# A two-layer attention and mixture-of-experts kernel whose first experts' stage issues no dummy products on TensorE

## The reference, cut to what matters

```python
logits = xf @ router_w.T                      # 256 features -> 64 experts
scores = softmax(logits); topk_w, topk_idx = top_k(scores, 8)
...                                           # each expert collects at most CAP = 64 token slots
gate = einsum('ech,ehf->ecf', xb, w_gate)     # h = 256, f = 96
up   = einsum('ech,ehf->ecf', xb, w_up)
hmid = silu(gate) * up
yb   = einsum('ecf,efh->ech', hmid, w_down)
out  = zeros.at[slot_token].add(yb[dest] * topk_w)
...
x = x + s * silu(out)                         # layer 0 ends; layer 1 works on the same x
```

## Time and profile before

| | us |
|---|---|
| median of 3 executions | 1122.3 |
| lowest and highest of them | 1118.9, 1123.69 |
| the profiled execution, its time | 1118.6 |
| its span in the trace | 1116.6 |
| TensorE busy | 988.5 |
| VectorE busy | 851.8 |
| ScalarE busy | 667.4 |
| GpSimd busy | 544.5 |
| mean granted TensorE clock | 0.955 |

### The profile page before, as it was taken

The page is one execution under the profiler, slowest core; times in us unless marked ns, Lnnn a source line. Parts: engine busy times, 40 slices in busy tenths (PEclk is TensorE's granted clock), DMA queues, the critical chain, the costliest instruction groups (busy, mean ns, idle before and its releaser), DMA issues.

```text
span 1116.6 us, 22230 instructions
## 1 busy us (share of the span) xinstructions
PE 988.5 (89%) x6749; PEld 650.3 (58%) x6749; DVE 851.8 (76%) x2241; ACT 667.4 (60%) x1739; POOL 544.5 (49%) x538
## 2 busy tenths in 40 slices
PE   3967879856999999999999999999988899999985
PEld 2535533334565676666666766767654678885443
DVE  4787548846798779768668899999856887775777
ACT  1733425524768766977866666666646877775332
POOL 0489556621755565544444444544521345553774
PEclk9987989976999999999999999999999999999997
DMA  9979699879562466121211001210049345553443
GB/s 340 338 220 368 161 261 289 287 259 279 81 166 76 115 117 144 36 74 39 63 53 39 32 8 39 91 39 1 1 135 322 98 134 145 147 139 92 133 131 95
DMA packets 97023, 155.99 MB, mean 140 GB/s; under 512 B 12272, under 2 KB 67312, under 8 KB 94096
## 3 DMA queue, kind: packets, MB, share of 16 engines
q1 hardware_dynamic: 77184, 115.42, 31.5%
q0 software_dynamic: 19728, 39.21, 15.8%
HBM read 104.84 MB, written 45.02 MB: 134 GB/s over the span
## 4 chain that ended last, share of the span: by engine, by line
PE 56%; DVE 14%; ACT 9%; issue 6%; DMA 4%; POOL 4%; DVEq 4%; POOLq 1%; ACTq 1%; SPq 0%
PE ps L1094 9%; PE ps L1266 6%; PE ps L1158 5%; PE ps L1146 5%; PE ps L1108 5%; PE ps L1126 3%; PE ps L1212 3%; PE ps L1229 3%; ACT arena L1522 2%; PE ps L1284 2%; PE ps L991 1%; PE ps L1136 1%; PE ps L1008 1%; PE ps L1256 1%; DVE x_sb L1909 1%
## 5 line engine op out<-in xcount | busy, mean ns | idle before, releaser
L2354 POOL TENSOR_TENSOR arena<-arena 128x512 f32<-128x512 f32 x128 | 174.6, 1421 | 98.3 <-ACT arena L1499 98.2
L1094 PE MATMUL ps<-arena 128*128 128x512 f16 x768 | 178.4, 383 | 1.3 <-ACT arena L1499 1.3
L2359 POOL TENSOR_TENSOR arena<-arena 128x512 f32<-128x512 f32 x64 | 67.7, 1057 | 176.0 <-DVE arena L2003 176.0
L2396 POOL DMA_INDIRECT wvo<-xn_d,idx x79 | 75.7, 958 | 113.5 <-PE ps L1256 96.4
L1094 PEld LDWEIGHTS ps<-arena 128*128 128x128 f16 x768 | 75.3, 98 | 93.9 <-ACT arena L1499 3.5
L1522 ACT ACTIVATE arena<-arena 128x128 f32<-128x128 f32 x256 | 99.2, 390 | 38.6 <-DVEq L1998 38.6
L1498 ACT ACTIVATE arena<-ps 64x512 f32<-64x512 f32 x128 | 76.0, 593 | 52.0 <-DVE arena L1971 48.4
L1158 PE MATMUL ps<-wvo,arena 128*128 128x256 f16 x768 | 95.1, 276 | 6.0 <-DVE s_sb L2023 3.2
L1146 PE MATMUL ps<-arena 128*128 128x192 f32 (+1 forms) x512 | 94.5, 328 | 2.4 <-DVE arena L2009 2.4
L1971 DVE TENSOR_TENSOR arena<-ps,wvo 128x512 f32<-128x512 f32 x128 | 84.7, 684 | 15.0 <-PE ps L1094 14.4
L1108 PE MATMUL ps<-wvo,arena 128*128 128x512 f16 x384 | 93.0, 379 | 2.9 <-issue 1.5
(11 more groups left out here) (296 smaller groups left out, 2193.6 us busy)
## 6 DMA issues: line engine op xcount, KB each, us to landing
arena<-wqk_d SPq DMA_DIRECT2D x16, 1024.0 KB, 5.8
arena<-in_wgu SPq DMA_DIRECT2D x32, 384.0 KB, 3.8
y_d<-wvo SPq DMA_DIRECT2D x79, 128.0 KB, 2.4
z_d<-wvo SPq DMA_DIRECT2D x8, 1024.0 KB, 4.3
z_d<-wvo SPq DMA_DIRECT2D x2, 4096.0 KB, 25.6
arena<-in_wdn SPq DMA_DIRECT2D x32, 192.0 KB, 5.3
arena<-z_d SPq DMA_DIRECT2D x12, 512.0 KB, 4.1
arena<-z_d POOLq DMA_DIRECT2D x12, 512.0 KB, 6.7
```

Of the source, the lines that this page charges most:

```text
L1094: last = pe.matmul(ps[s][:, :], wqk[gg][:, s * DC + c, w, hh * DH:(hh + 1) * DH], hx[bb][:, :, x, c * P:(c + 1) * P], start=(c == 0 and w ...
L2354: nc.gpsimd.tensor_tensor(qk_s[:, s], qk_s[:, s], sin, ALU.mult).then_inc(sin_done, 1)
```

## The change

`keep_clock` and its one call are deleted. Everything else is as before, on all engines: the same products, waits, transfers, buffers. In the kernel after, line numbers behind the deleted helper are 5 lower, and behind the deleted call 6 lower.

```diff
-            def keep_clock(bank, n):
-
-                for _ in range(n):
-                    pe.matmul(ps[bank][:, :], ones_bf[:, :], ones_bf[:, :].unsqueeze(1).to_broadcast([P, 4, P]), start=True, stop=True)
...
             def expert_turn(j):
 
                 upto(pe, hmT_rd, j - 1)
-                keep_clock(6, 2)
                 upto(pe, hm_ready, j)
                 pe.transpose(ps[6][0:F0, 0:P], hm0[:, j % 4], ident[:, :]).then_inc(hmT_ps, 1)
```

## The result

| | before | after |
|---|---|---|
| median, us | 1121.07 (4 executions) | 1143.42 (4 executions) |
| all executions, us | 1118.9, 1119.85, 1122.3, 1123.69 | 1128.13, 1141.65, 1145.19, 1146.23 |
| mean granted clock of these of after | | 0.933, 0.918, 0.911, 0.913 |
| profiled execution: time, span | 1118.6, 1116.6 | 1141.65, 1139.7 |

With all four, median over median is 1.020. The forecast was 1146 us, between 1116 and 1150, slower.

What follows compares the result with a forecast made beforehand. The prediction took TensorE to bound the kernel, at its clock's pace: low after the stall, 105.9 us replace 81.4 (+24.5), tail -1.0, net +23.5; 1122.3 + 23.5 = 1146 us, range 1116 to 1150.

Steps and rivals of the forecast that it cites:

- The clock decides, not the removed work: Experts' stage: the edit's price is which clock the rounds get, not the 64 products removed; net +23.5 us.
- Once low, it stays low until the stage ends: Experts' stage after the stall: TensorE's clock stays at 0.50 to the end; 1146 us, chance 0.53.
- the prediction's own sign: Test on the profile after: a granted clock going to and fro in the experts' stage would mean rival B.
- rival B: Experts' stage: the clock returns, but late; 1124 to 1138 us, say 1130; chance 0.19.
- Prices of rounds: Experts' stage, rounds without dummies: one unit 4.03 us low, 2.42 high; double rounds 8.6 low, 6.4 high.
- The dummies before the stall: Six rounds before the wait for pair 8's rows: removing 12 dummies gains 0 us, bounds 0 and -0.4.
- The sum from there: From the restart after the stall to the end of TensorE's stage work: 105.9 us at the low clock, before 81.4.
- The tail: From TensorE's stage end to the last scatter: 2.3 us before, about 1.4 at the slow pace, so -1.0.
- This goes to the end undiminished: Behind the experts' stage everything hangs on the last scatter, so the net +23.5 us reaches the kernel's end.
- Rival A: Experts' stage: the clock returns 9.07 us after the restart and stays; -6.9 us, 1115 us; chance 0.20.
- rival C: Experts' stage: the clock returns but DMA or VectorE takes up the freed time; 1120 to 1123 us; chance 0.08.
- once high, no stretch of the stage comes near the pause that brought it down: Argument for Rival A: behind the restart, no stretch resembles the 144.90 to 151.11 pause, so the clock holds.

Runs made afterwards that it cites:

- e4: Kernel before with its two dummies only in turns 13 to 24, the twelve rounds of the double stretch: median 1127.8 us, ratio 1.006.
- e5: Kernel before, its dummies moving the same 512 columns over 32 rows and 32 weight columns in place of 128 and 128: ratio 1.037.
- e8: Kernel after, unchanged, ten more executions on another chip: median 1167.8 us against 1149.9 for the kernel before, ratio 1.010.
- e1: Kernel after plus 26 filling products with ones in TensorE's idle stretch at the end of round 4: median 1137.2 us, ratio 1.018.
- e3: Kernel before with one dummy per pair in place of two: median 1116.7 us, ratio 0.9986.
- e6: Kernel after plus 26 filling products at the end of round 4 and two dummies before the middle unit's product in six double rounds: ratio 1.0005.
- e10: Kernel before plus 26 filling products in round 4's idle stretch, one dummy per pair, two before the middle unit's product in six rounds: 1112.1 us, ratio 0.9945.

## Why the prediction was right, point by point

**The clock decides, not the removed work: right.** e4 and e5 show it from both sides: with dummies put back in 12 of the 32 pairs the clock is held there, with dummies as long on a sixteenth of the array it is at 0.50 throughout. e8 shows the total time following the clock from one execution to the next.

**"Once low, it stays low until the stage ends": right in kind, too strong.** In the profiled execution it rose at 179 and at 209 us and fell again 10 and 3.5 us later; that saved 4.0 us in the double rounds (rounds 12 to 23 took 226.62 - 178.99 = 47.6 us, 51.6 forecast). In e8 it did stay low. By the prediction's own sign ("if the clock goes to and fro, B") the profiled execution is in part rival B, at nearly the forecast's price, since only 13.4 of 102.6 us were high; and the fastest execution, 1128.1 us, lies in B's 1124 to 1138. What lifts the clock in rounds that look alike in the timeline is open; it differs from execution to execution, and so does the time.

**Prices of rounds: right.** One unit, low level: 4.03 forecast, 4.07 measured. Double, low: 8.60 and 203.27 - 194.59 = 8.68. Double, high, no dummies: 6.4 and 187.02 - 180.59 = 6.43. One unit, high, no dummies: 2.42 forecast; 2.40 where the transfers had slack (e4), **2.81 where they had not** (e1).

**The dummies before the stall: 0 to -0.4 us.** TensorE's first transposes behind the pause start at 150.74, before at 151.11: -0.4, the lower bound. Pair 8's rows were indeed asked for earlier (L2321 at 137.59, before L2327 at 138.08). But the prediction took them for what ends the pause, and in this trace the transfer that TensorE waits for is `short_d`, which landed at 150.15; in e8 it waits for both, 5.14 and 1.52 us. The two are close, and the prediction named only one. The sum from there: 105.9 us forecast, 252.76 - 150.74 = 102.0 measured. The tail took 1.7 us where I had 1.4. Together +19.6 at the last scatter instead of +23.5.

**"This goes to the end undiminished": right, and the total was met by luck.** The total of the profiled pair, +23.1, meets the forecast of +23.5 only because 3.5 us came later, in unchanged work, where the profiled execution of the kernel before was quicker than every later one (881.7 us against 883.0 to 887.7). The stage itself cost 19.6. Here two errors cancel.

**Rival A** rested on two claims that fell. Its -6.9 contained 3.0 us for rounds with one unit, 0.30 each. In e1 they were slower than with dummies, as long as the weights' transfers were behind; in e3, which came nearer to A's case, six rounds took 170.19 - 154.16 = 16.0 us, 2.67 each, with DMA at 1.04, so little came back there either. What I had put into rival C at 0.08 is a part of A. And "once high, no stretch of the stage comes near the pause that brought it down" was wrong: the clock fell behind waits of 1.1 to 1.3 us among rounds without dummies (after, e1, e6), far shorter than the pause.

**Of the rule in the Trainium skill, "TensorE: Matmul & The Clock Gate", section "What's actually happening"**, that sustained activity releases the throttle, the runs show the limit: 28.8 us without a gap in the kernel after passed at 0.51, and 120.6 busy of 120.7 us in e5 at 0.50. To be busy in the profile is not enough.

## What to carry to other kernels

Before you delete work that computes nothing, ask what clock the rest will get: multiply the neighbouring rounds by the low clock's rows, not only the deleted instructions by theirs. If such filling is needed, put it where TensorE waits anyway (a pause before a transfer, a wait for VectorE), and trim it elsewhere: here that added half a percent (e10) to a device worth 1.3 to 2.0%. And a faster round is worth something only if its transfers can follow: look for the stretch where DMA is full before you count its gain.

## What the hardware showed that I had not expected

Products on 32 rows and 32 weight columns take TensorE as long as full ones (0.96 us for two at the low level) but do not bring the clock back: 0.50 to 0.51 from 147 us to the end of the stage in e5, and the time grows by 3.7%. The clock can also fall in the midst of work, behind waits of 1.1 to 1.3 us, and then stay down for tens of microseconds (53.8 in e1) in which TensorE never waits; yet after another wait of 1.16 us it stayed up (e1). And the same program needs 1120 us on one chip and 1150 on another; the last stretch, in which the shared expert's products run and rows are gathered from DRAM, is where the traces part: from the last down product of the routed experts to the end 99 us in the profile of before, 120 in e6's. Why is open.
